# Routed expert steps on one core: TensorE runs the first products of a tile ahead of the transposes of the inputs of the tile after it

## The reference

```python
weights, indices = _gate(xt, gate_w)                    # 4 of 16 experts for each of 2048 tokens
combine = jnp.einsum('tk,tke->te', weights, one_hot(indices, E))
h1 = jnp.einsum('td,eid->tei', xt, W1)                  # d = 256, i = 176
h3 = jnp.einsum('td,eid->tei', xt, W3)
g = jax.nn.silu(h1) * h3 * combine[:, :, None]
y = jnp.einsum('tei,edi->td', g, W2)
```

## Time and profile before

| what | us |
|---|---|
| median of 3 runs | 1061.2 |
| the three runs | 1061.2, 1052.15, 1081.17 |
| the profiled execution | 1050.47 |
| its span from first to last instruction | 1048.7 |
| routed stage, first X to last O, within the span | about 815 to 1003 |

### The profile page before, as it was taken

One profiled execution on the slowest core, in us unless ns is written; L12 is line 12 of the kernel. 1 busy time (PEld: TensorE's weight loads), 2 busy tenths in 40 slices (PEclk: granted clock), 3 DMA queues, 4 the chain that ended last, 5 costly groups with the idle time before them and its releaser, 6 DMA issues.

```text
span 1048.7 us, 19959 instructions
## 1 busy us (share of the span) xinstructions
PE 870.9 (83%) x6996; PEld 740.5 (71%) x6996; DVE 733.7 (70%) x1648; ACT 568.5 (54%) x1062; POOL 666.4 (64%) x641
## 2 busy tenths in 40 slices
PE   4563799999999999999999997737990899999920
PEld 4552477888878888788888786637880798998920
DVE  5674676878788787978788885586880466666656
ACT  1201387878778788887887886522320344444410
POOL 3513378888888878797888885504666255555544
PEclk9776799999999999999999999857995899999965
DMA  5654243223432233422325135233222333333254
GB/s 183 227 189 95 44 138 80 79 60 68 117 103 58 68 82 84 145 54 74 86 56 159 40 99 211 81 78 92 97 101 108 106 116 110 122 119 119 88 217 184
DMA packets 66332, 113.69 MB, mean 108 GB/s; under 512 B 16981, under 2 KB 43484, under 8 KB 64268
## 3 DMA queue, kind: packets, MB, share of 16 engines
q1 hardware_dynamic: 47337, 71.21, 25.7%
q10 hardware_dynamic: 11987, 23.36, 6.3%
q0 software_dynamic: 6912, 17.84, 4.4%
HBM read 46.45 MB, written 41.68 MB: 84 GB/s over the span
## 4 chain that ended last, share of the span: by engine, by line
PE 59%; DVE 12%; DMA 12%; POOL 7%; issue 5%; ACT 3%; SPq 0%; POOLq 0%; DVEq 0%; ACTq 0%
PE bank L661 13%; PE bank L663 11%; PE bank L662 11%; DMA slots<-h,slot_i 8%; PE bank L834 7%; PE bank L1038 6%; PE bank L811 4%; POOL p_lo L1858 3%; POOL turns L1836 2%; PE bank L1010 2%; PE bank L897 2%; DVE turns L1197 1%; DVE turns L1198 1%; DVE h L1545 1%; DMA rows_f<-turns 1%
## 5 line engine op out<-in xcount | busy, mean ns | idle before, releaser
L1858 POOL TENSOR_TENSOR p_lo<-p_f,p_hi 128x512 f16<-128x512 f32 x256 | 324.5, 1279 | 62.2 <-ACT p_f L1602 61.7
L1224 DVE TENSOR_REDUCE nmax<-bank 128x1 fp32r<-128x512 f32 x256 | 174.3, 686 | 98.1 <-PE bank L811 94.3
L1599 ACT ACTIVATE p_hi<-bank,log_up 128x512 f16<-128x512 f32 x256 | 176.2, 688 | 110.4 <-PE bank L663 101.2
L1602 ACT ACTIVATE p_f<-bank,log_up 128x512 f32<-128x512 f32 x256 | 175.4, 685 | 6.8 <-POOL p_lo L1858 6.8
L834 PEld LDWEIGHTS bank<-vals,p_hi 128*128 128x128 f16 x2048 | 110.4, 98 | 51.3 <-issue 23.6
L834 PE MATMUL bank<-vals,p_hi 128*128 128x66 f16 x2048 | 138.7, 194 | 7.6 <-POOL p_lo L1858 7.0
L661 PE MATMUL bank<-qk 128*128 128x512 f32 x256 | 122.6, 479 | 8.2 <-issue 7.8
L1204 DVE TENSOR_TENSOR qk<-rows_f,qk 128x512 fp32r<-128x512 f32 (+1 forms) x128 | 127.4, 995 | 2.0
L1836 POOL TENSOR_TENSOR turns<-turns 128x512 f32<-128x512 f32 x64 | 89.3, 1398 | 55.1 <-DVE turns L1198 55.1
L834 PE MATMUL bank<-vals,p_lo 128*128 128x66 f16 x1024 | 121.1, 193 | 0.0
L811 PE MATMUL bank<-qk 128*128 128x512 f32 x256 | 103.4, 407 | 6.1 <-DVE nmax L1224 4.0
(11 more groups left out here) (231 smaller groups left out, 2106.1 us busy)
## 6 DMA issues: line engine op xcount, KB each, us to landing
rows_f<-turns SPq DMA_DIRECT2D x64, 256.0 KB, 3.9
slots<-pad ACTq DMA_DIRECT2D x4, 2880.0 KB, 10.2
h<-slots SPq DMA_DIRECT2D x80, 144.0 KB, 2.1
w_hi<-parts SPq DMA_DIRECT2D x16, 512.0 KB, 7.8
rows_f<-kl_f SPq DMA_DIRECT2D x32, 192.0 KB, 3.0
w_raw<-in_w ACTq DMA_DIRECT2D x4, 1408.0 KB, 12.1
h_dram<-h_hl SPq DMA_DIRECT2D x3, 1024.0 KB, 4.8
qk<-lat_st SPq DMA_DIRECT2D x16, 192.0 KB, 4.2
```

The source lines that it names most:

```text
L1224: dve.tensor_reduce(nmax[:, k % MAXES:k % MAXES + 1], max_bank[q % 2][:], AX_X, ALU.max, negate=True)\
L1599: act.activation(p_hi[:, u % TB, :], score_bank[u % 2][:], ACT.Exp, bias=log_up[:, 0:1], scale=SCALE)
L1602: act.activation(p_f[:, u % 2, :], score_bank[u % 2][:], ACT.Exp, bias=log_up[:, 0:1], scale=SCALE)\
L1858: pool.tensor_tensor(p_lo[:, u % TB, :], p_f[:, u % 2, :], p_hi[:, u % TB, :], ALU.subtract).then_inc(s_pl, 1)
```

## The change

The block that issues I of tile n+2 is moved ahead of the block that issues X of tile n+3, in PE's body alone. Each block keeps its own waits and its own count. PE's order in step n becomes I (n+2), X (n+3), T (n+1), O (n). No instruction is added or removed, and the bodies of the other four engines stay as they are.

```diff
@@ expert_position on PE
+                if within(n + 2, SLOT_TILES):
+                    m, par = n + 2, j % 2
+                    expert = experts[place + 2]
+                    pe.wait_ge(e_lo, m + 1)
+                    if static(m) and m < 2:
+                        pe.wait_ge(z_g, 2 * NT)
+                    else:
+                        pe.wait_ge(e_g, m - 1)
+                    inner_products(par, par, lambda k: w_hi[:, bass.ds(expert, 1), k, :].rearrange("p a n -> p (a n)"),
+                                   lambda k: w_lo[:, bass.ds(expert, 1), k, :].rearrange("p a n -> p (a n)")).then_inc(e_h, 1)
                 if within(n + 3, SLOT_TILES):
                     m, jm = n + 3, (j + 3) % CYCLE
                     pe.wait_ge(ld_s[jm], 16 * (over(m, CYCLE) + 1))
...
                     mm.then_inc(e_x, 1)
-                if within(n + 2, SLOT_TILES):
-                    m, par = n + 2, j % 2
-                    expert = experts[place + 2]
-                    pe.wait_ge(e_lo, m + 1)
...
```

## The result

The changed kernel is slower. In the first comparison (four runs of each) its median is 1081.88 us (1074.05 to 1098.21), that of the kernel before 1069.88 (1052.15 to 1081.17), and the ratio is 1.0256, with a 95% interval of 1.0196 to 1.0315. Both intervals lie above 1 and both hold 1.02, so that it is slower is shown, and whether by more than two per cent isn't. A ratio here isn't that of the medians beside it (1.011 in the first comparison): it leaves out runs in a slower state that executions of either kernel can fall into, while a median takes all runs. The two profiled executions took 1050.47 and 1074.87 us, spans 1048.7 and 1073.0: 24.3 us between the spans.

The account below looks back on a forecast made before the run. PE's own routed step of 2.27 us was taken as the bound. Stall 22.6 + filling 3 - return 2.1 = 23.5 us, giving 1074 on the profiled run or 1084.7 on the median; forecast 1082, range 1064 to 1097.

Parts of the forecast that it names:

- the base: Whole kernel: 23.5 us added to the profiled 1050.5 gives 1074, to the median of the runs shown 1084.7; forecast 1082.
- the filling: Routed stage's first steps: less cover before I of tiles 1 and 2, 2.2 us more, taken as 3 (2 to 6).
- The chain: Routed stage, X's start through hi, lo, address work and weight load to I's first product: 1.59 us.
- The mechanism: Routed steps: chain 1.59 us against cover 1.30, PE idle 0.29 a step, 2.56 instead of 2.27, 22.6 us over 78.
- The covers: Routed stage's other queues: later silu, g and cast cost nothing; slack 1.1 us before T, 0.8 before O.
- The return: Routed stage, O of tile 0 to tile 76: stalls from cast waiting for stores vanish, giving back 2.1 us.
- The sum: Whole kernel: 22.6 + 3 - 2.1 = 23.5 us more, 2.2% on the profiled execution.
- the longer chain: Rival, routed steps: hi, lo or address work slower by 0.1 in all, 8 us more, 1093; 6 in 100.
- the smaller stall: Rival, routed steps: address work ahead or load hidden, stall 0.15 to 0.18, 13 to 15 us, 1072 to 1076; 14 in 100.
- A sign that I named wrongly: Routed stage: PE idle some 0.3 us before line 661 once in each step, named as DVE x_hl or issue.
- the row with which I argued that the clock would hold: 665 to 670 us, 4.40 busy of 5.00 at clock 1.00; against the falling-clock rival, 39 us more, 1124, 6 in 100.
- The rule weighed: I's weight load: pulled ahead past a waiting sequencer, the stall would be 0.18 a step, 14 us instead of 22.6; judged unlikely.

Follow-up runs that it names:

- E2: Changed kernel with I split: four products using hi alone first, the wait for lo before the last two; ratio to the kernel before 1.0029, step 2.26 us.
- E4: Changed kernel with X moved, PE order I, T, X, O; step 2.78 us, profiled run 1114.0 us.
- E7: Kernel before with an extra subtraction of the same size on VectorE just before lo; step 2.27 us, profiled run 1052.2 us.
- E3: Kernel before with I split: four products using hi alone first, the wait for lo before the last two; median 1051.14 us, ratio 0.9975.
- E1: Changed kernel again, no edit, longer comparison: median 1078.71 us over 7 runs, kernel before 1052.33 over 24, ratio 1.0229.
- E5: Changed kernel with X moved last, PE order I, T, O, X; step 3.65 us, profiled run 1162.3 us.
- E9: Changed kernel plus a one-load fp32r product of 2 columns ahead of the wait for lo, so the address is worked out earlier; step 2.38, profiled run 1059.4 us.
- E6: Changed kernel with an extra subtraction of the same size on VectorE just before lo; step 2.89 us, profiled run 1105.4 us.
- E10: Changed kernel with X before I in the steps up to n = 0 only; step 2.56, filling 7.09, profiled run 1069.5 us.

## Why the prediction's mechanism was right, and where its time was wrong

Two steps failed: the base on which the difference was put to give a time, and the price of the filling, above all of the clock in it. The chain and the length of the step held.

**The mechanism** was right, and so was each link of the steady steps. Forecast and measured: X to hi 0.42 and 0.42; hi to lo 0.41 and 0.42; lo 0.42 and 0.42; lo's end to the load 0.23 and 0.23; load to first product 0.11 and 0.11. Step forecast 2.56, measured 2.56. E2, E4 to E7 show that it is this chain and not the order: it goes when lo leaves it, grows with it, and scales with the cover.

**The covers** called safe were safe: the weight loads of T and O show one wait each in the whole stage, of 0.2 and 0.3 us.

**The return** of 2.1 us was right: the stretch from O of tile 0 to O of tile 76 grew by 19.8, and 76 x 0.29 - 2.1 = 19.9. The waits of cast are gone too, as forecast. But the 2.1 came from a single execution, and E3 and E7, in the order of before, lost 1.8 and 1.2 us of it (stretches of 172.8 and 173.5). So it is no fixed cost of the old order, and that the forecast hit it so closely is partly luck.

**The filling** was the term mis-sized: 5.0 us measured (4.2 by the trace of E1), 3.3 forecast, that is 3 and the first 0.29 of the steady steps, which falls into the same stretch. The step that failed is "with more idle time it may rise later", put at 0.8 us. The idle time itself was right. Rows of the changed kernel around I of tile 1 and of tile 2:

```profile
818.48 0.63 PE L1020 MATMUL bank<-ident,h 128*128 128x128 f32 x2
...
820.24 0.29 PEld L661 LDWEIGHTS bank<-w_hi,x_hl 128*128 128x128 f32 x1 [1.53 <-issue]
...
820.69 0.50 PE L662 MATMUL bank<-w_lo,x_hl 128*128 x1
...
822.59 0.64 PE L897 MATMUL bank<-ident,g_s 128*88 128x128 f32 x2
...
824.37 0.49 PE L662 MATMUL bank<-w_lo,x_hl 128*128 x1
```

A pair of transposes takes 0.42 at this clock and products follow each other by 0.29. So PE stands from 818.90 to 820.40, 1.50 us where 1.37 was forecast, and from 823.01 to 824.08, 1.07 where 1.16 was. Two things are left. X of tile 1 is in the filling now, 0.42 us of it. In the kernel before, PE ran it while it waited for lo of tile 0, and the forecast gave it nothing:

```profile
815.48 1.25 PE L1010 MATMUL bank<-ident,h 128*128 128x128 f32 x4 [27.91 <-DMA h<-slots]
```

The rest, 5.0 - 2.57 - 0.42, some 2.0 us by this estimate, is work at 1.2 GHz that the kernel before did at 2.4: its clock came up at about 822, that of the changed kernel at 829.4.

**The sum** was 23.5 us, and the spans differ by 24.3. As a ratio it is 1.0224, inside both measured intervals.

**The absolute time** failed. I had put two sums side by side, 1074 on the profiled execution and 1084.7 on the median of three runs, and leaned to the upper. The step that failed is "I expect the changed kernel's median nearer the upper figure". That 1082 is so near the first median (1081.88) is luck, since the base of that comparison had moved too. Over its four runs the kernel before had 1069.88, and the ratio put on that base is 1069.88 x 1.0256 = 1097.3, just outside my range. Over the 24 runs of E1 it had 1052.33, near its profiled 1050.47, and 1052.33 x 1.0229 is 1076.4, below my figure. So 1082 fits neither base: with the sum of 23.5 it would need a base of 1058.5. Three runs spread over 29 us said that the median was no anchor; the profiled execution was the better one, and the range should have been put up as a difference, 19 to 31 us, on a stated base. Two bounds were slips as well: 1097 follows from none of the sums (the longer chain on the upper base is 1093), and the smaller stall on the median starts at 1074, not 1072.

**A sign that I named wrongly.** I wrote that PE idle time of 0.3 us would show before line 661. On PE's rows it doesn't (1.8 us in 160 us of steady steps), since modelled ends cover it. It shows on the weight loads (36.3 us over 79 of them) and in the count of matmuls. For the same reason the row with which I argued that the clock would hold, 88% busy, was weaker than it looked: rows of that kind overstate. E5 settles it better.

**The rule weighed** in the prediction didn't shorten the wait. Over the steady steps the load starts 0.18 to 0.26 us after lo's end in the changed kernel, with a median of 0.23, and 0.05 to 0.06 in E9, never before it.

## What to carry to other kernels

When a block moves ahead on one engine, write down for each loop-carried value what the engine does between giving the input away and needing the result back, before and after. That cover against the chain's length gave the new step to within a few hundredths in the changed kernel and in E2, E4, E5 and E6. A pipeline's first steps need a sum of their own, with what each engine did before while it waited and with the clock that it has there. And a difference should be put on a stated base. Links to count that no busy row shows: the sequencer's register work between a wait and the instruction it guards, and the weight load behind it. If the guarded instruction has parts that need less, put the wait before the part that needs more.

## What the runs showed of the hardware

- From lo's end to the dependent weight load it took 0.05 us where the address had been worked out before, and 0.23 with the address instruction, of 0.14, in between (E9 and the changed kernel).
- PE at 14.18 us busy of 20.00, in gaps of over 1 us in every step of 3.65, kept the granted clock at 1.00 (E5). At the start, after 11.8 us without a matmul, the changed kernel with gaps of 1.5 and 1.1 us stayed at 0.50 until about 829.4; the kernel before and E10, without these gaps, were at 1.00 from 822.
- Where the traces differ before the routed stage, it is in the shared expert's stretch, in which GpSimd scatters the tokens by indirect DMAs. The scatters end at about 810 us in all traces of these four: before, after, E1 and E4. The shared expert's last product starts at 787.2, 802.5, 827.7 and 834.8. In the first two X of tile 0 still has to wait for its load, 27.9 and 11.8 us, so a late shared expert costs them nothing; in the other two it delays the stage. Waits of that stretch (722 to 812 us), of the kernel before and then of E4:

```profile
PE bank L661 <- DVE g_s L1449: 1.2, 2, 0.6
```

```profile
PE bank L661 <- DVE g_s L1449: 30.9, 5, 15.1
...
ACT x_hl L1744 <- remote: 19.4, 5, 8.9
```

The longest wait of the same kind is 0.6 us in one trace and 15.1 in the other. Some of these waits run on though the work they need is over: in E4 ScalarE's silu (line 1750) starts at 780.17, while the products it reads end at 774.54 by their rows, and the profile puts the wait down to "remote".

```profile
774.05 0.49 PE L663 MATMUL bank<-ws_hi,x_hl 128*128 128x352 f32 x1
...
780.17 0.32 ACT L1750 ACTIVATE sl<-bank 128x176 f32<-128x176 f32 x1 [8.94 <-remote]
```

What does it stays open; none of the runs was made for it, and the long runs of the first comparison have no trace. Late shared experts stand in traces of the changed kernel (E1) as in those of E2 (last product at 819.6) and E4. The readings of steps and fillings don't rest on it, since they are taken inside the routed stage.
